# A fused attention and GRU kernel on one core: W_hh loaded in twelve pieces of 32 partitions, eight of them earlier; V's projections of the first example and W_v's low part moved behind the first scores

## What is computed

```python
# layer 0: conditioned attention, 16 heads of 32 features
scale, shift = split(cond @ W_emb + b_emb)
xn = rms_norm(x, g_norm) * (1 + scale) + shift
q, k, v = split(xn @ W_qkv)
q, k = rms_norm(q, g_q), rms_norm(k, g_k)      # within each head
o = softmax(q @ k.T * 32 ** -0.5) @ v
x = x + o + o @ W_out

# layer 1: a GRU over the 256 positions, h starts as cond
gi = x_t @ W_ih + b_ih
gh = h @ W_hh + b_hh
r, z = sigmoid(i_r + h_r), sigmoid(i_z + h_z)
n = tanh(i_n + r * h_n)
h = (1 - z) * n + z * h
x = x + (all h)
```

## Time and profile before

| | |
|---|---|
| runs | 1756.86, 1757.49, 1756.93 us; median 1756.93 |
| the profiled execution | 1759.35 us, span 1757.2 us |
| mean granted TensorE clock | 0.989 |
| TensorE busy | 1692.2 us, 96% |
| VectorE, ScalarE, GpSimd busy | 1127.5, 978.4, 391.8 us |
| chain that ended last | PE 93%, DVE 2%, POOL 2%, DMA 1% |
| DMA issues of W_hh | four of 512 KB, four of 256 KB |

### The profile page before, as it was taken

One profiled execution on the slowest core, in us unless ns is written; L12 is line 12 of the kernel. 1 busy time (PEld: TensorE's weight loads), 2 busy tenths in 40 slices (PEclk: granted clock), 3 DMA queues, 4 the chain that ended last, 5 costly groups with the idle time before them and its releaser, 6 DMA issues.

```text
span 1757.2 us, 68343 instructions
## 1 busy us (share of the span) xinstructions
PE 1692.2 (96%) x28717; PEld 1382.2 (79%) x28717; DVE 1127.5 (64%) x4056; ACT 978.4 (56%) x3584; POOL 391.8 (22%) x480
## 2 busy tenths in 40 slices
PE   6899999999999999599999999999999999999986
PEld 5688888888888887378888888888888888888864
DVE  4776767776777766256666666666666666666664
ACT  3777777777777776034444444444444444444444
POOL 4633333334343343001111111111111111111111
PEclk8999999999999999899999999999999999999999
DMA  5032222211212112463233333333333333333320
GB/s 206 23 121 54 57 52 57 57 49 49 49 49 49 50 38 74 121 104 81 72 83 78 82 81 73 79 82 80 80 74 83 78 78 84 77 79 75 72 66 14
DMA packets 211450, 127.77 MB, mean 73 GB/s; under 512 B 78956, under 2 KB 193336, under 8 KB 211144
## 3 DMA queue, kind: packets, MB, share of 16 engines
q1 hardware_dynamic: 211144, 123.40, 28.2%
HBM read 73.01 MB, written 50.33 MB: 70 GB/s over the span
## 4 chain that ended last, share of the span: by engine, by line
PE 93%; DVE 2%; POOL 2%; issue 1%; ACT 1%; DMA 1%; SPq 0%; POOLq 0%; DVEq 0%; ACTq 0%
PE ps L680 37%; PE ps L651 19%; PE ps L467 14%; PE ps L514 6%; PE ps L550 5%; PE ps L494 4%; PE ps L529 4%; PE ps L475 2%; PE ps L440 1%; DMA xscr<-x1s 1%; PE ps L537 1%; POOL rq L1191 1%; POOL wo_l L1220 0%; DVE v L926 0%; DVE v L931 0%
## 5 line engine op out<-in xcount | busy, mean ns | idle before, releaser
L680 PE MATMUL ps<-whh,hT 128*32 128x192 f32 x16384 | 720.3, 326 | 16.6 <-DVE hT L952 16.1
L680 PEld LDWEIGHTS ps<-whh,hT 128*32 128x32 f32 x16384 | 587.4, 110 | 124.1 <-DVE hT L952 80.4
L651 PE MATMUL ps<-wih,x1T 128*32 128x256 f32 x6144 | 384.5, 381 | 0.7 <-ACT x1T L1048 0.7
L1138 ACT ACTIVATE v<-ps 128x128 f32<-128x128 f32 x512 | 139.1, 272 | 439.6 <-PE ps L680 439.6
L1251 POOL TENSOR_TENSOR outG<-hG,GI 128x128 f32<-128x128 f32 x256 | 117.2, 458 | 935.7 <-DVE hG L945 935.7
L651 PEld LDWEIGHTS ps<-wih,x1T 128*32 128x32 f32 x6144 | 240.8, 111 | 67.8 <-issue 2.2
L926 DVE SCALAR_TENSOR_TENSOR v<-v,ps 128x64 f32<-128x64 f32 x512 | 113.3, 221 | 275.7 <-ACT v L1138 275.7
L1030 ACT ACTIVATE P<-ps,nmx 128x256 f32<-128x256 f32 x512 | 236.5, 482 | 2.5 <-DVE nmx L744 2.5
L1146 ACT ACTIVATE v<-v 128x64 f32<-128x64 f32 x512 | 131.3, 256 | 106.6 <-DVE v L931 106.6
L1191 POOL TENSOR_TENSOR rq<-msq,mh 128x16 f32<-128x16 f32 x64 | 185.6, 2900 | 5.3
L744 DVE TENSOR_REDUCE nmx<-ps 128x4 f32<-128x1024 f32 x128 | 156.2, 1221 | 29.4 <-PE ps L494 29.4
(11 more groups left out here) (96 smaller groups left out, 1935.4 us busy)
## 6 DMA issues: line engine op xcount, KB each, us to landing
gscr<-nat SPq DMA_DIRECT2D x96, 256.0 KB, 2.6
GI<-gscr SPq DMA_DIRECT2D x128, 192.0 KB, 3.7
xb<-in_x_dram SPq DMA_DIRECT2D x16, 512.0 KB, 3.3
xres<-in_x_dram SPq DMA_DIRECT2D x32, 256.0 KB, 2.9
xscr<-x1s SPq DMA_DIRECT2D x32, 256.0 KB, 2.0
xblk<-x1s SPq DMA_DIRECT2D x128, 64.0 KB, 2.6
GI<-xscr SPq DMA_DIRECT2D x128, 64.0 KB, 2.8
out_dram<-outG SPq DMA_DIRECT2D x128, 64.0 KB, 2.9
```

What stands on the lines that cost most here:

```text
L651: last = pe.matmul(F[G % 2][q, n], x1T[:, tt % 2, j, c, :], wih[:, c, g * D + 256 * half:g * D + 256 * half + 256], start=(c == 0), stop=( ...
L680: last = pe.matmul(ps[32 * j:32 * j + 32, q, 0:192], hT[:, 32 * c:32 * c + 32], whg[:, c, :, 128 * j + 64 * q:128 * j + 64 * q + 64], star ...
L1138: s.activation(v_rz[:, q, :], ps[:, q, 64:192], ACT.Tanh, scale=0.5).then_inc(s_tr, 1)
```

## The change

Three things are changed.

1. W_hh comes in twelve loads (`load_whh(j, k)`), each to 32 partitions and one third of the columns, 256 KB. The source is `"(c f) n -> f c n"`, so both sides lead with 32. Eight of them (k = 0 and 1, over the high parts of W_q and W_k) are issued at the top of example 15's pass, once the last q and k are projected (`projected` at 6 x 15 + 4), ahead of the stores of example 14's first half. The other four (k = 2, over W_v's high part) stay where the eight loads were. The first step waits for 12 x 16 instead of 8 x 16.
2. In the setup TensorE projects q's half 1 (into bank 6) directly behind q's half 0, transposes both halves of k, x and q, makes `scores(0)`, and projects V (into banks 5 and 4) behind that. VectorE copies V instead of ScalarE and makes W_v's low part behind the normalization of q.
3. ScalarE copies and squares q's half 1 before the first exponentials, and GpSimd makes the low part of the second example's x (`x_low(1, 0)`) before it adds the identity to `wout`.

```diff
-PASS = [("rows", 1, 0), ("rows", 1, 1), ("project", 0, 1, 0)]
+PASS = [("project", 0, 1, 0), ("rows", 1, 0), ("rows", 1, 1)]
...
+            def load_whh(j, k):
+                g = (k + 2) % 3
+                sp.dma_start(whh[32 * j:32 * j + 32, :, k * D:k * D + D],
+                             W_hh[128 * j:128 * j + 128, g * D:g * D + D].rearrange("(c f) n -> f c n", c=KC)).then_inc(s_lwh, 16)
...
+                if b == NB - 1:
+                    sp.wait_ge(s_qkv, 6 * b + 4)
+                    for j in range(4):
+                        for k in range(2):
+                            load_whh(j, k)
                 if b:
                     store_x1(b - 1, 0)
                     load_residual(b, 0)
...
-                    for c in range(KC):
-                        w = W_hh.rearrange("(j c f) n -> c j f n", j=4, c=KC)[c]
-                        sp.dma_start(whh[:, c, 0:D], w[:, :, 2 * D:3 * D]).then_inc(s_lwh, 16)
-                        sp.dma_start(whh[:, c, D:3 * D], w[:, :, 0:2 * D]).then_inc(s_lwh, 16)
+                    for j in range(4):
+                        load_whh(j, 2)
...
-            pe.wait_ge(s_nrm, 1)
-            project(0, 0, 2, 2, lambda: turn(0, 0, 1, 0))
-            project(0, 1, 2, 5, lambda: turn(0, 1, 1, 1))
...
+            passed(("project", 0, 1, 0))
+            turn(0, 0, 1, 0)
+            turn(0, 1, 1, 1)
             passed(("rows", 1, 0))
             pe.wait_ge(s_qk0[1], 1)
             turn(0, 0, 0, 0)
             passed(("rows", 1, 1))
             scores(0)
-            passed(("project", 0, 1, 0))
+            project(0, 0, 2, 5)
+            project(0, 1, 2, 4)
...
+            def keep_first_v(i):
+                v.wait_ge(s_qkv, 5 + i)
+                v.tensor_copy(V[:, 0, i, :], ps[:, 5 - i, :]).then_inc(s_v, 1)
...
-            for c in range(KC):
-                wq_low(2, 2, c, c + 1)
             squares(0, 1, 1)
             normalize(0, 0, 1)
...
-            normalize(0, 0, 0)
             keep_turned_k(1)
             affine(1, 0, BANK["rows", 1, 0])
+            normalize(0, 0, 0)
+            for c in range(KC):
+                wq_low(2, 2, c, c + 1)
...
             maxima(0, 1)
+            keep_first_v(0)
             affine(1, 1, BANK["rows", 1, 1])
+            keep_first_v(1)
             recips(0)
...
-            keep_v(0, 0)
-            keep_v(0, 1)
+            keep_raw(0, 1, 0)
+            square_raw(0, 1, 0)
+            x_high(1, 0)
```

More of the change, by code:

```diff
@@ L52 @@
     PASS += [("recips", _p)] + [_x for _slot in slots(_p) for _x in _slot if _x]
-BANK = {p: 6 if p[0] in ("project", "out") else 4 if p == ("rows", 1, 1) else 7 for p in PASS}
+BANK = {p: 6 if p[0] in ("project", "out") or p == ("rows", 1, 1) else 7 for p in PASS}
 EMPTIED = {}
@@ L223, in cond_resid_kernel @@
                              "pv", "o", "o_high", "o_low", "out_proj"))
-        s_ev = {k: sem(f"bank{k}_empty") for k in (4, 6, 7)}
+        s_ev = {k: sem(f"bank{k}_empty") for k in (6, 7)}
         s_qk0 = [sem("q_kept0"), sem("k_kept0")]
@@ L482, in scores @@
                     pe.wait_ge(s_qk0[0], 1)
-                    pe.wait_ge(s_v, 1)
                 elif p % 4 == 0:
@@ L504, in turn_p @@
                     pe.wait_ge(s_v, 2)
-                    emptied(pe, ("rows", 1, 1))
                 for j in range(4):
@@ L673, in _ @@
                         else:
-                            pe.wait_ge(s_lwh, 128)
+                            pe.wait_ge(s_lwh, 192)
                     elif (q, c) == (1, 0) and t:
@@ L996, in keep_raw @@
                 bank = BANK["project", b, i, g]
-                s.wait_ge(s_qkv, 6 * b + k - 4 * b + 1 if b else 6)
+                s.wait_ge(s_qkv, 2 * b + k + 1)
                 s.wait_ge(s_qT, k - 1)
@@ L1019, in keep_v @@
             def keep_v(b, i):
-                bank = BANK["project", b, i, 2] if b else (2, 5)[i]
-                s.wait_ge(s_qkv, 6 * b + 5 + i if b else 4 + i)
+                bank = BANK["project", b, i, 2]
+                s.wait_ge(s_qkv, 6 * b + 5 + i)
                 if b >= 2 and i == 0:
                     s.wait_ge(s_pv, 4 * (b - 1))
-                s.copy(V[:, b % 2, i, :], ps[:, bank, :]).then_inc(s_ev[bank] if b else s_v, 1)
+                s.copy(V[:, b % 2, i, :], ps[:, bank, :]).then_inc(s_ev[bank], 1)
             def exps(p, h):
@@ L1079, in _ @@
                          scale=gqs).then_inc(s_qk0[0], 1)
-            x_high(1, 0)
             exps(0, 0)
@@ L1083, in _ @@
             x_high(1, 1)
-            keep_raw(0, 1, 0)
-            square_raw(0, 1, 0)
             s.wait_ge(s_wi, KC)
@@ L1210, in _ @@
             rsqrt(0, 0, 0)
+            x_low(1, 0)
             g_.wait_ge(s_lwo, 16)
@@ L1214, in _ @@
                 g_.tensor_tensor(w, w, ident, ALU.add).then_inc(s_wi, 1)
-            x_low(1, 0)
             x_low(1, 1)
```

## The result

| | before | after |
|---|---|---|
| median, runs on one chip | 1757.21 us (1756.86 to 1759.95, 4 runs) | 1736.43 us (1735.17 to 1736.92, 4 runs) |
| ratio, 95% interval | | 0.9877 [0.9860, 0.9894] |
| the profiled execution | 1759.35 us, span 1757.2 us | 1735.17 us, span 1733.4 us |
| mean granted TensorE clock | 0.989 | 0.995 |

The change makes the kernel faster by 1.23%, 21.6 us of 1757.21 by the ratio; 21.1 were forecast, and the time forecast was 1735.8 us.

A forecast was written before the change was run, and what follows sets the result against it. TensorE was taken as the bound, 93% of the chain of waits, so only its waits could give much. Passage 18.5 us (16.1 wait, 2.4 clock) plus setup 2.6 made 21.1: 1756.93 to 1735.8 us, range 1733.5 to 1741.0.

The forecast's parts named there:

- The store's wait: Before the GRU, the last example's first-half store lands in 2.0 us instead of 13.54; TensorE goes on 16.1 us earlier.
- the passage: From the last example's attention into the GRU: store's wait and clock at the restart together give 18.5 us.
- The clock at the restart: At the GRU's start TensorE keeps full clock: 0.66 us on the transposition and 1.70 on the first products, 2.4 together.
- Rival 1: At the GRU's start the clock falls all the same: 1738.2 us; chance 0.13.
- Eight early loads: W_hh loads issued at 664.85 us, when the last q is projected, land between 671 and 685 us.
- Rival 3: W_hh's loads to 32 partitions are slow and hold up the store, from 4.6 us a load; up to 1787.7 us; chance 0.05.
- the fourth case: W_hh's loads keep 103 GB/s, ending at 685 and 697 us; time as forecast, chance within the forecast's 0.70.
- The setup: The reordered start of the kernel brings the second scores forward by 2.6 us, between 1.6 and 3.9.
- V's products as the bound: In the setup, V's projections bound the second scores at 45.05 us, 0.4 us behind the exponentials.
- the low part: In the setup, W_v's low part beside GpSimd may take twice 2.48 us: second scores at 47.3, gain only 1.6 us.
- the slow clock: In the setup, TensorE's 2.3 us idle before q's transposition brings half clock on scores and V, costing 1.7 us.
- Rival 2: The setup gives nothing, its delays adding up or GpSimd's stretch growing: 1738.4 to 1740.8 us; chance 0.09.

The follow-up runs named there:

- Experiment 2: The kernel before with only the twelve new W_hh loads, eight early and four late, and the old setup: 1740.03 us, ratio 0.9892.
- experiment 12: The changed kernel once more, unedited: 1735.74 us, ratio 0.9873.
- Experiment 4: The changed kernel with its twelve W_hh loads, eight still early, each from a source led by four to 128 partitions: 1743.10 us, ratio 0.9916.
- experiment 3: The changed kernel with all twelve 32-partition W_hh loads at the old, late place, none early: 1737.51 us, ratio 0.9881.
- Experiment 1: The changed kernel with W_hh loaded as before, in eight late loads over 128 partitions, so only the new setup: 1755.77 us, ratio 0.9986.
- experiment 7: The changed kernel with W_v's low part back between the sums of k's halves: 1739.06 us, ratio 0.9893.
- experiment 6: The changed kernel with V's first eight matmuls before q's transposition and GpSimd's identity sums behind the first scores: 1733.86 us, ratio 0.9863.

## Why the prediction was right, step by step

**The store's wait: right.** It lands in 2.0 us as forecast, and TensorE goes on without idle time. Experiment 2 puts the passage at 19.0 us by the ratio and 17.7 by the medians; 18.5 were forecast. In the two profiles it is 20.1 us (the first step starts at 729.98 instead of 753.44, of which 3.4 come from the setup). The 1.6 beyond the forecast are the output projection of 2.99 us, which experiment 12 shows to be a matter of the execution and not of the change: with 4.58 us for it, the passage there is 18.4 us shorter than before (659.78 to 729.95, against 664.83 to 753.44).

**The clock at the restart: right**, 0.50 and 1.63 us in the profiles against 0.66 and 1.70 forecast. The 0.44 us that the forecast took for a transposition at full clock was the distance to the start of the next piece; where its end is waited for, it is 0.60. Experiment 4 is the counterpart: with the store landing 6.42 us after its issue, the first 192 products took 12.48 us. Rival 1 is out.

**Eight early loads: on time, but not needed.** They end near 673 us, inside the 671 to 685 forecast. The Trainium skill, "SBUF — State Buffer", section "Door 1: The DMA port swizzle", gives 32 partitions half of the ports and about 218 GB/s; the trace agrees, with 195 to 199 GB/s in single microseconds of experiment 3 and a full DMA share beside it. Rival 3 is out: twelve such loads take 3.1 MB / 0.197 = 16 us, 1.3 us a load where the rival needed 4.6, and even late they are through before the store.

**"That case changes nothing": wrong.** This is the one step that failed outright, the fourth case, counted inside the forecast's chance. It took the loads' rate as the only thing at stake: in the old form they would end at 685 and 697 us. It left out what it had itself read in the earlier trace rows, that such loads hold the queue while they are issued. They hold it 13.3 us, everything behind them moves, the late four leave 7.8 us later, and the kernel is 5.6 us slower than with the new form even if that is issued late. The case didn't occur, so the number stayed right.

**The setup: right in size, in part for another reason and in part by luck.** Experiment 1 gives 2.5 us, 2.6 were forecast. `msq` takes 0.21 us and q is normalized at 37.39 (37.15 forecast). The first scores come at 39.49, 1.0 later than forecast: 0.3 because q's transposition starts at 37.54, 0.7 because the clock fell already there. The second come at 46.92, within the 45.05 to 47.3 forecast, 2.0 us earlier than before. The forecast had V's products as the bound, 45.05 at full clock and 1.7 more at half clock. In the first profile that is so, by 0.5 us; but in experiment 12, at full clock, V is done near 45.1 and the exponentials behind W_v's low part set the start, 45.63. So V and the low part are two bounds within half a microsecond of each other, and the forecast, which had the low part only as its lower end, took the slow clock and the low part for alternatives where both were there. `msq` of q's half 1 comes 1.75 us earlier (50.89), not 2.6.

In the first profile the setup's gain is 1.8 us where the chain goes back to TensorE (69.72 instead of 71.53) and 3.4 by the last q (661.46 instead of 664.83, by the first load's issue after and the end of the earlier trace rows). The further 1.6 is again the clock: before, the half clock lay on the path there, where 32 products took 1.94 us and the scores behind them 1.81; after, they took 1.08 and 1.07, and the half clock lay at 65 to 68 us, under GpSimd's chain. No term of the forecast held this. The 32 products take 1.08 us in ten of the twelve profiles with the new setup, 1.70 and 1.93 in experiments 1 and 7, and 1.94 in both with the old setup. So it is a gain of most executions, not of all, and the profiles of the changed kernel give the setup 3.4 and 5.0 us. Rival 2 is out by experiment 1, narrowly: its interval ends at 0.9 us.

What stays open: why the granted clock fell at the last example's first output projection in nine profiles without filling and not in three others; whether the source's leading dimension or the 32 partitions of a load make the new form fast; and whether experiment 6's 2.6 us over the changed kernel holds; the ratios' intervals, [0.9849, 0.9878] and [0.9860, 0.9894], overlap.

## What to carry to other kernels

When a small store lands late, look at what stands ahead of it in its queue: a load whose source is led by a short dimension moves at the rate of few DMA engines and also holds the queue at its issue. There are two ways out, another form of the load and an earlier place, and they don't add: here early issue took 12.7 us off the kernel with the old form and nothing that could be measured off the one with the new form. Try the form first (here 32 on both sides instead of 4 on the source): alone it brought nearly all, and it leaves the queue free for what stands behind. And when a forecast says of a case that it changes nothing, check each thing that the case does, not only the one that was priced.

## What the runs showed of the hardware

- Loads of 256 KB to 32 partitions, led by 32 on both sides: 176 GB/s over 12 us, 195 to 199 GB/s in single microseconds, with the DMA engines shown busy 0.91 and 1.06 to 1.08. A busy share alone doesn't tell a fast transfer from one at half speed; GB/s beside it does.
- Eight loads led by four on the source took 13.2 to 13.3 us to issue, and stores of 128x4x32 behind them 2.0 us each instead of 0.6.
- Four VectorE products of 128x512 took 2.48 to 2.51 us beside short GpSimd instructions, 3.56 us beside one long one and 4.08 to 4.36 beside a low part and four additions; the additions took 3.05 to 3.50 us beside them and 1.69 to 1.72 without them. A GpSimd instruction that takes 0.2 us otherwise took 0.57 or 2.16 under the same four products, at starts 0.17 and 0.40 us behind theirs.
- The Trainium skill, "SBUF — State Buffer", section "SBUF: two separate sides", describes one lock for the ports that VectorE and GpSimd share, held for a whole instruction by whoever starts first. The 2.16 us, and the low part of x at 1.27 us when it starts first and 1.71 when it starts second, agree with it. In experiment 7 the short instruction ended at 26.94, just behind the first of the four products (a quarter of 2.51 us from 26.20, so near 26.83): by this reading it got in between two products.
- Idle times of TensorE of much the same length had different ends: 2.34 us before q's transposition was followed by half clock in the first profile of the changed kernel, 2.18 by full clock in experiment 12; and the 1.72 us before the last example's first output projection were followed by 2.99 us for its products in one and 4.58 in the other.
